# Second cross attention of a gated two-layer stack: the transposes of the probabilities as two 64-query halves in row tiles, and a new order within a burst

## The reference

```python
xn = _layernorm(x, ln_gamma, ln_beta)
q = (xn @ w_q).reshape(B, SQ, NUM_HEADS, DIM_HEAD)
kv = context @ w_kv
k, v = jnp.split(kv, 2, axis=-1)
...
scores = jnp.einsum('bqhd,bkhd->bhqk', q * SCALE, k)
attn = jax.nn.softmax(scores, axis=-1)
out = jnp.einsum('bhqk,bkhd->bqhd', attn, v).reshape(B, SQ, INNER)
out = out @ w_out + b_out
return out * jnp.tanh(gate[0])
```

## Time and profile before

| | us |
|---|---|
| median of 3 runs | 2561.95 (2558.16 to 2563.05) |
| profiled execution, its own time | 2568.06 |
| span of the profiled execution | 2566.4 |
| first scores of the second cross attention, from the span's start | 1258.7 |
| TensorE busy, of the span | 2326.1 |
| VectorE busy | 1818.8 |
| ScalarE busy | 871.8 |

### The profile page before, as it was taken

How to read it: one execution, slowest core, us unless ns; L and a number is a source line. 1 busy time by engine, 2 the same in 40 slices (tenths; PEclk the granted TensorE clock), 3 DMA queues, 4 the chain that set the end, 5 groups by cost and what they waited for, 6 DMA issues and landing times. The chain is left out here.

```text
span 2566.4 us, 46634 instructions
## 1 busy us (share of the span) xinstructions
PE 2326.1 (91%) x16954; PEld 1639.0 (64%) x17040; DVE 1818.8 (71%) x5138; ACT 871.8 (34%) x2075; POOL 200.1 (8%) x283
## 2 busy tenths in 40 slices
PE   3878788699999999999899999999888999999998
PEld 1555556445575565667555655656568888888887
DVE  4868678597747657654577777776577878787785
ACT  1757477415024023032255555454331111111110
POOL 1523411101011011010000000000000000000000
PEclk7999899899999999999899999999989999999999
DMA  7435323300000000200100000000030000000000
GB/s 189 69 68 88 48 47 47 132 0 1 1 1 1 1 1 1 99 1 1 44 1 1 1 1 1 1 1 1 1 132 1 2 0 8 0 8 0 0 9 9
DMA packets 43513, 65.30 MB, mean 25 GB/s; under 512 B 5056, under 2 KB 36160, under 8 KB 42688
## 3 DMA queue, kind: packets, MB, share of 16 engines
q1 hardware_dynamic: 43328, 62.88, 10.5%
HBM read 54.48 MB, written 8.39 MB: 24 GB/s over the span
## 5 line engine op out<-in xcount | busy, mean ns | idle before, releaser
L2089 PEld LDWEIGHTS banks<-work,big 128*128 128x128 f32 x2048 | 251.4, 195 | 9.5 <-issue 1.9
L2089 PE MATMUL banks<-work,big 128*128 128x128 f32 x2048 | 253.3, 278 | 1.7 <-ACT work L2180 1.5
L1358 PE MATMUL banks<-big,work 128*128 128x256 f32 x1024 | 242.1, 381 | 0.8
L1788 ACT ACTIVATE work<-banks,work 128x512 f32<-128x512 f32 x256 | 175.2, 691 | 171.5 <-DVE work L1877 171.4
L1260 PE MATMUL banks<-big,work 128*128 128x512 f32 x512 | 224.7, 600 | 4.4 <-DVE work L1481 4.4
L2196 ACT ACTIVATE work<-banks 128x512 f32<-128x512 f32 x128 | 76.4, 597 | 437.2 <-PE banks L2089 437.2
L1358 PEld LDWEIGHTS banks<-big,work 128*128 128x128 f32 x1024 | 195.6, 191 | 37.6 <-issue 0.3
L771 PE MATMUL banks<-ident,work 128*128 128x128 f32 x1024 | 166.0, 287 | 53.4 <-ACT work L888 43.9
L888 ACT ACTIVATE work<-work 128x512 f32<-128x512 f32 x256 | 182.9, 716 | 88.2 <-DVE work L1026 88.2
L1877 DVE TENSOR_REDUCE work<-banks 128x2 f32<-128x1024 f32 x128 | 150.5, 1218 | 82.5 <-PE banks L1683 82.3
L1026 DVE CUSTOM_DVE_ANT_0 work<-banks,big 128x512 f32<-128x512 f32 x256 | 173.4, 686 | 47.8 <-issue 41.2
(11 more groups left out here) (207 smaller groups left out, 4119.6 us busy)
## 6 DMA issues: line engine op xcount, KB each, us to landing
wc<-parts SPq DMA_DIRECT2D x128, 128.0 KB, 6.9
parts<-big SPq DMA_DIRECT2D x16, 384.0 KB, 2.5
big<-in_bias SPq DMA_DIRECT2D x4, 1024.0 KB, 10.5
big<-in_B_val SPq DMA_DIRECT2D x8, 512.0 KB, 6.7
big<-in_B_out SPq DMA_DIRECT2D x1, 4096.0 KB, 20.1
big<-in_D_downT SPq DMA_DIRECT2D x1, 4096.0 KB, 12.8
big<-in_D_up SPq DMA_DIRECT2D x1, 4096.0 KB, 22.2
wc<-in_ctxT SPq DMA_DIRECT2D x1, 2048.0 KB, 7.5
```

What stands on the lines that cost most here:

```text
L1358: last = eng.matmul(XB[qt][:, 0:D], spread[:, w % NG, qt * P:(qt + 1) * P], w_out[:, w, :], start=(w == 0), stop=(w == GE - 1))
L1788: eng.activation(prob[:, n % NS * PAIR + j, :], SB[n % 2][:, j, :], ACT.Exp, bias=low[:, n % NS, j:j + 1], accum_out=rowsum[:, n % NS, j:j ...
L2089: last = eng.matmul(HP[n % 2][:, q * P:(q + 1) * P], down[:, kc * ELO + n * NJ + q, :], xnT[par][:, kc, :], start=(kc == 0), stop=(kc == K ...
```

## The change

The eight 128x128 transposes of a step become sixteen: each 128x128 block of `prob` is turned as two halves of 64 queries, which use the upper and the lower 64 rows of the array. The two halves write to different banks: `TB[0]` now holds the first 64 queries of both heads for all keys, `TB[1]` the last 64. So ScalarE copies the first halves of both heads and VectorE the second halves, still 512 values per partition each, in runs of 64 instead of 128. `pT` has the same content under a flattened index. The signals of a step still are two, now both at its end.

The order of a burst changes on all three engines. On TensorE the transposes of n-2 go ahead of the scores of n and n+1. On VectorE the copy of n-2 goes ahead of both `lowest`. On ScalarE the copy of n-2 goes ahead of the first exponential. The transposes of n-1 stay where they were, behind keys or values.

```diff
-    pT = carve(m, "big2")(2 * PAIR, QT, S)
+    pT = carve(m, "big2")(2 * PAIR * QT, S)
...
-    CW = 512
+    CW, HALF = 512, P // 2
...
                     for j in range(PAIR):
                         for kt in range(QT):
-                            last = eng.transpose(TB[j][:, kt * P:(kt + 1) * P],
-                                                 prob[:, n % NS * PAIR + j, kt * P:(kt + 1) * P], ident[:, :])
-                        last.then_inc(t_made.sem, 1)
+                            for half in range(2):
+                                r, at = slice(half * HALF, (half + 1) * HALF), (j * QT + kt) * HALF
+                                last = eng.transpose(TB[half][:, at:at + HALF],
+                                                     prob[r, n % NS * PAIR + j, kt * P:(kt + 1) * P], ident[r, r])
+                                if j == PAIR - 1 and kt == QT - 1:
+                                    last.then_inc(t_made.sem, 1)
...
                 for b, t, u, n in bursts():
-                    scores(b, t, u, n)
                     if n >= 2:
                         turn_probs(n - 2)
+                    for i in range(2):
+                        scores(b, t, u, n, i)
...
-                    eng.activation(pT[:, tile % 2 * PAIR, :, qt * P:(qt + 1) * P],
-                                   TB[0].rearrange("p (k q) -> p k q", q=P), ACT.Copy).then_inc(pt0_ready.sem, 1)
+                    eng.activation(pT[:, tile % 2 * PAIR * QT:(tile % 2 + 1) * PAIR * QT, qt * P:qt * P + HALF],
+                                   TB[0].rearrange("p (k q) -> p k q", q=HALF), ACT.Copy).then_inc(pt0_ready.sem, 1)
...
-                    spread_probs(n, 0)
                     if n >= 2:
                         take_probs(n - 2)
+                    spread_probs(n, 0)
                     spread_probs(n, 1)
...
-                    eng.tensor_copy(pT[:, tile % 2 * PAIR + 1, :, qt * P:(qt + 1) * P],
-                                    TB[1].rearrange("p (k q) -> p k q", q=P)).then_inc(pt1_ready.sem, 1)
+                    eng.tensor_copy(pT[:, tile % 2 * PAIR * QT:(tile % 2 + 1) * PAIR * QT, qt * P + HALF:(qt + 1) * P],
+                                    TB[1].rearrange("p (k q) -> p k q", q=HALF)).then_inc(pt1_ready.sem, 1)
...
+                    if n >= 2:
+                        take_probs(n - 2)
                     lowest(n)
                     lowest(n + 1)
-                    if n >= 2:
-                        take_probs(n - 2)
```

More of the change, by code:

```diff
@@ L1669, in values, with scores @@
                     last.then_inc(v_made.sem, 1)
-                def scores(b, t, u, n):
-                    if u == 0:
+                def scores(b, t, u, n, i):
+                    if u == 0 and i == 0:
                         eng.wait_ge(k_ready.sem, k_ready.at(b, t + 1))
                         eng.wait_ge(q_ready.sem, q_ready.at(b, t + 1))
[L1676 to L1685, removed]
+                    if n + i >= 2:
+                        eng.wait_ge(p_ready.sem, p_ready.at(0, 2 * (n + i - 1)))
+                    qt = 2 * u + i
+                    for c in range(2):
+                        for j in range(PAIR):
+                            r = slice(j * DK, (j + 1) * DK)
+                            last = eng.matmul(SB[i][:, j, c * 256:(c + 1) * 256], qT[r, t % 2, qt * P:(qt + 1) * P],
+                                              kT[r, t % 2, c * 256:(c + 1) * 256], start=True, stop=True)
+                    last.then_inc(s_made.sem, 1)
                 def turn_probs(n):
@@ L1707, in weigh @@
                             last = eng.matmul(FB[0][j * DK:(j + 1) * DK, :], vtok[:, kt, h * DK:(h + 1) * DK],
-                                              pT[:, t % 2 * PAIR + j, kt, :], start=(kt == 0), stop=(kt == QT - 1))
+                                              pT[:, (t % 2 * PAIR + j) * QT + kt, :], start=(kt == 0), stop=(kt == QT - 1))
                     last.then_inc(av_made.sem, 1)
```

## The result

The changed kernel takes 2544.05 us (median of 4 runs, 2536.87 to 2544.86) against 2562.5 us for the kernel before: a ratio of 0.9924, 95% interval 0.9907 to 0.9941, so 15 to 24 us less. The forecast was 2535 in a range of 2524 to 2554.

What follows compares the result with a forecast made beforehand. TensorE was taken to set the pace, with a chain over VectorE and ScalarE close behind. Gains and losses by kind of tile summed to -26.5 us, taking the median from 2562 to 2535 us, range 2524 to 2554.

Steps and rivals of the forecast that it cites:

- tiles with `project`: 12 tiles that also project the previous sequence: 19.84 to 18.7 us, less 1.15 each, -13.8 us.
- the first sequence: Its four tiles with values and the norm's work as well: taken at -0.6 us each, -2.4 us.
- the tail: Last tile and tail: less than half of 8.1 us of waits for VectorE's copy taken as gained, -3.3 us.
- the last two tiles: Two last tiles without values: VectorE's copy goes first, 13.8 in place of 16.64 us, -2.85 each, -5.7 us.
- A pair of half transposes passes every 0.058 us: Transposes on TensorE: 8 pairs a step take 0.464 in place of 0.872 us, 52 us less work over 128 steps.
- Changes of form: TensorE switching between whole array and row or column tiles: eight a tile for five, +0.5 us a tile, 16 over 32.
- The values' chain: VectorE and ScalarE work up to the values' copy before the weighing: 12 tiles at 16.7 us, -0.23 each, -2.8 us.
- rival 4: Clock falls in the new waits of up to 1.5 us in 16 tiles: +10 to +20 us on the forecast; chance 0.03.
- The first tile: First burst pair: transposes wait for the normalised step 0, and scores 2 and 3 now stand behind them, +1.5 us.
- Rival 1: Transpose pairs do not pass side by side: 0.87 us a step, about +8 us, 2570; chance 0.11.
- rival 2: Transpose pairs pass at 0.08 us, or copies are dearer: 0.64 a step, 14 us given back, 2549; chance 0.12.
- rival 3: Values' chain costs less than added up: 16 tiles gain up to 1 us more, sum near -40, 2522; chance 0.1.

Runs made afterwards that it cites:

- e3: Changed kernel with the loop over the halves outside, eight transposes in the upper row tile, then eight in the lower: 2562.02 us, 1.0013 of the kernel before.
- e2: Kernel before with its whole-array 128x128 transposes, but in the new order on all three engines: 2562.28 us, 1.0015 of the kernel before.
- e5: Changed kernel with the transposes of odd steps, which stand alone between whole-array work, 128x128 again: 2545.56 us, 0.9929 of the kernel before.
- e10: Changed kernel with the parts of the next sequence's norm moved behind both `lowest` on VectorE: 2555.28 us, 0.9975 of the kernel before.
- e9: Changed kernel, unedited, run once more: 2544.6 us, 0.9921 of the kernel before.
- e6: Changed kernel with the values' copy ahead of ScalarE's third exponential and, in burst u = 1, VectorE's copy between the two `lowest`: 2527.61 us, 0.9858 of before.
- e8: Kernel of e6 with the very first transposes and their copies behind scores 2 and 3, as before the change: 2526.86 us, 0.985 of the kernel before.
- e1: Changed kernel's half transposes in the kernel before's order on all three engines (scores, then transposes n-2): 2547.76 us, 0.9948 of the kernel before.

## Why the prediction was right, and where it was off

The direction, the range and the mechanism hold; the amount was 18.5 us in place of 27, and 19.9 in the stage of the profile in place of 26.5. Two terms make up nearly all of the difference, the tiles with `project` (3.1 us) and the first sequence (3.5); the tail gave 1.6 less and the last two tiles 1.8 more than forecast. Point by point:

- *A pair of half transposes passes every 0.058 us.* Right: 0.062. e3 shows that the side-by-side passage is all of the gain, and e2 that the order alone gives none. The figure for loads of the Trainium skill (TensorE: Matmul & The Clock Gate, LDWEIGHTS), 0.107 us for 128 columns, would have set 0.107 a pair. It does not hold for these loads: two of 128 columns in two row tiles went by every 0.062 us.
- *Changes of form, 0.15 to 0.20 us each, three more a tile.* Right within the rows: e2 shows 0.31 a tile where these prices give 0.25, e5 0.25 where 0.25 was expected. Between transposes and scores there is no such cost: the scores start 0.06 us after the last pair, one pair's distance.
- *The values' chain becomes the bound of tiles with values.* Right: 16.69 against 16.7, wait 1.16 (0.72 with `turn_x`); e4 removes one exponential and the tile gives back exactly that.
- *Tiles with `project`*: 18.93 in place of 18.7, and 19.36 in the four that have the root's parts. I had not set these apart, though they took 20.2 before, too. -10.7 in place of -13.8. Of the 0.2 a tile, 0.13 is the pair distance (eight times 0.062, 0.496 a step, for 0.464). The rest is in the changes of form: with the work of a tile at the prices above and this distance, 1.43 of the 18.93 us are left for eight of them, where I had 1.35 (an estimate).
- *Last two tiles*: 13.74, as worked out (13.8); -7.5 in place of -5.7, since one of them had a slow weighing before.
- *The term that was mis-sized most is the first sequence*, tiles 2 to 5: -2.4 forecast, +1.1 measured (73.9 to 75.0 us). I had taken a guess of -0.6 a tile beside the norm. The trace of the kernel before shows what the guess passed over. TensorE was already waiting there, 4.0 us in four waits for VectorE's copy behind both `lowest`, so a chain was the bound of these tiles and less work on TensorE could gain little:

```profile
1284.69 1.06 PE L1695 MATMUL banks<-ident,work 128*128 128x128 f32 x8 [0.98 <-DVE big L1895]
...
1303.00 1.07 PE L1695 MATMUL banks<-ident,work 128*128 128x128 f32 x8 [1.06 <-DVE big L1895]
...
1321.51 1.06 PE L1695 MATMUL banks<-ident,work 128*128 128x128 f32 x8 [1.26 <-DVE big L1895]
...
1339.10 1.06 PE L1695 MATMUL banks<-ident,work 128*128 128x128 f32 x8 [0.70 <-DVE big L1895]
```

In the changed kernel the weighing waited 1.8 to 2.1 us in each, 7.7 in all, for the values' copy; the norm's parts on VectorE lengthen that chain (e10). After one such wait the clock fell to its lower level for 3.4 us, which cost 1.7 us (e4 has shorter waits, no such spell, and 1.7 us less). This is rival 4, which I had given 3%: it came about, but in one tile of the first sequence (two in e9) and not in the 16 that it was priced for. I had held against it that a wait of 1.78 us occurs in the last tiles. But the next wait of that kind in the same trace is followed by the lower clock, and that is the slow weighing of the kernel before:

```profile
1815.62 1.07 PE L1695 MATMUL banks<-ident,work 128*128 128x128 f32 x8 [1.77 <-DVE big L1895]
1816.62 5.35 PE L1707 MATMUL banks<-big,wc 128*64 128x512 f32 x16
```

- *The first tile* is +1.9 (forecast +1.5).
- *The tail*: -1.7 in place of -3.3, a share I had only guessed, and of too large a sum: of the 8.1 us of waits that I put there and "in small pieces", 4.0 are those of the first sequence above.

Rival 1 (no overlap) is refuted by the trace and by e3; rival 2 (0.08 a pair) too; rival 3 (a shorter chain) is refuted by the 1.16 us wait and the 16.69 us of the value tiles.

Three versions are better than the changed kernel, and their whole times do not tell them apart: e4, the changed kernel with the values' copy moved up on ScalarE (0.9867), e6 (0.9858) and e8 (0.985). In the profiled stage e6 is the shortest (564.4 us, e8 568.9, e4 572.3).

## What to carry to other kernels

Price a row-tiled rewrite from the kernel's own rows: the distance of pairs, the length of loads, and what each change of form costs; then set it beside work that is row-tiled already, since a lone group between whole-array work keeps little (here 0.12 us of 0.37). When TensorE gets faster, follow the chain to the copy that its next wait names and look at what stands ahead of that copy: one exponential moved behind it was worth 9.6 us in the profiled stage, half as much as the whole rewrite (19.9). And count apart the stretches that have extra work, and look whether TensorE waits in them already: the first five tiles lost 3.0 us, where I had counted on a gain of 0.9.

## What the runs showed of the hardware

- TensorE does not keep strictly to the order of its list across row tiles, against what I wrote of all engines ahead of the prediction. In e3 a score matmul started before three transposes that were ahead of it, and eight transposes of one row tile followed by eight of the other took 0.80 us from first to last start instead of 0.93.
- Loads of the transposes (128 columns, float32) go by every 0.06 us, in the changed kernel in two row tiles at once, ordinary float32 loads of the same shape every 0.11.
- The clock fell to its lower level (1.2 GHz) for 3.4 us after some waits of TensorE and not after others of the same length: after 2.01 us and not after 2.08 in the changed kernel, after 2.08 and 2.02 in e9, after 1.40 (and 0.59 more) in e1, after 1.77 in the kernel before. It never fell after the waits of 0.72 and 1.16 us in the twelve value tiles of the changed kernel.
